# Expert stages that start with their first block, a different split of the routing, and linear attention in column halves

## The reference

```python
x = x + tanh(g_xattn[0]) * L0_xattn(layernorm(x), ctx)   # softmax attention
x = x + tanh(g_ffn[0])   * L0_ffn(layernorm(x))          # 8 experts, 2 of them per token, hidden 128
x = x + tanh(g_xattn[1]) * L1_xattn(layernorm(x), ctx)   # linear attention, 16 heads of 16, 64 features each
x = x + tanh(g_ffn[1])   * L1_ffn(layernorm(x))          # causal attention, then 16 experts, 4 per token, hidden 256

def L0_ffn(x):
    w, idx = top_k(softmax(x @ router_w), 2); w = w / sum(w)
    return sum over the chosen e of w_e * (silu(x @ gate_e) * (x @ up_e)) @ down_e

def L1_xattn(query, key, value):            # per head, per sequence of 64 tokens
    q, k = relu(q @ Wqf.T), relu(k @ Wkf.T) * mask
    kv, k_sum = k.T @ v, sum(k)             # 64 x 16 and 64
    out = (q @ kv) / (q @ k_sum + 1e-8)
```

## Time and profile before

| | us |
|---|---|
| median of three runs | 2975.49 (2974.87 to 2975.98) |
| profiled execution, its own time | 2981.3 |
| its span | 2979.5 |
| softmax attention | 0 to 742.97 |
| experts of layer 0 | 742.97 to 1030.87 |
| linear attention | 1030.87 to about 1412 |
| causal attention | about 1412 to 2360.64 |
| experts of layer 1 | 2360.64 to 2979.5 |

### The profile page before, as it was taken

How to read it: one execution, slowest core, us unless ns; L and a number is a source line. 1 busy time by engine, 2 the same in 40 slices (tenths; PEclk the granted TensorE clock), 3 DMA queues, 4 the chain that set the end, 5 groups by cost and what they waited for, 6 DMA issues and landing times. The chain is left out here.

```text
span 2979.5 us, 57684 instructions
## 1 busy us (share of the span) xinstructions
PE 2334.0 (78%) x19856; PEld 1786.5 (60%) x19856; DVE 1904.6 (64%) x3843; ACT 1108.2 (37%) x2183; POOL 1109.1 (37%) x1111
## 2 busy tenths in 40 slices
PE   4999889973496179999389999989978429999990
PEld 2555555541475168888267777777766418888770
DVE  4788778760465267776487788788777344445753
ACT  1555555542242032332244444444333233333330
POOL 2344544446305300000155444444377551002616
PEclk7777777775599589999599999999989759999995
DMA  5455555422447511111333223322233363334744
GB/s 106 111 118 100 116 114 118 96 56 75 130 153 216 164 38 38 52 39 33 114 78 83 68 68 76 82 64 69 71 87 109 114 203 120 100 98 149 234 144 138
DMA packets 249894, 308.60 MB, mean 104 GB/s; under 512 B 46104, under 2 KB 203288, under 8 KB 249496
## 3 DMA queue, kind: packets, MB, share of 16 engines
q1 hardware_dynamic: 189016, 215.29, 27.5%
q0 software_dynamic: 26624, 58.79, 7.4%
q10 hardware_dynamic: 33984, 30.95, 3.1%
HBM read 122.00 MB, written 98.43 MB: 74 GB/s over the span
## 5 line engine op out<-in xcount | busy, mean ns | idle before, releaser
L645 DVE TENSOR_REDUCE soft_top<-soft_pa 128x4 fp32r<-128x1024 f32 x256 | 312.3, 1220 | 148.8 <-PE soft_pa L728 147.4
L1834 POOL TENSOR_TENSOR ca_qk<-ca_qk,ca_q_swap 128x512 f32<-128x512 f32 x160 | 250.7, 1567 | 397.4 <-DVE ca_q_swap L2001 396.9
L1038 POOL DMA_INDIRECT moe_yg<-moe_ys_rows,moe_slot_id x192 | 194.4, 1013 | 504.4 <-DMA moe_ys_rows<-moe_ys 399.4
L555 ACT ACTIVATE soft_prob<-soft_pb 128x1024 f32<-128x1024 f32 x256 | 262.3, 1024 | 275.0 <-PE soft_pb L712 274.8
L1213 PE MATMUL moe_pgu<-moe_w_hi,moe_xt_hi 128*128 x472 | 193.2, 409 | 42.1 <-DVE moe_xt_lo L1164 39.7
L1229 PE MATMUL moe_py<-moe_w_d,moe_at 128*128 x788 | 211.4, 383 | 0.0
L728 PE MATMUL soft_pa<-soft_rep 24*128 24x256 f32 x1024 | 164.1, 407 | 46.2 <-DVE soft_top L645 36.8
L1169 DVE TENSOR_TENSOR moe_act_f<-moe_silu,moe_pgu 128x256 f32<-128x256 f32 (+1 forms) x236 | 88.7, 376 | 170.5 <-ACT moe_silu L1089 170.3
L742 PE MATMUL soft_po<-soft_prob,soft_vaug 128*32 128x256 f32 x2048 | 190.5, 506 | 0.0
L712 PEld LDWEIGHTS soft_pb<-soft_rep 25*128 25x128 f32 x1024 | 98.8, 238 | 150.2 <-ACT soft_prob L555 79.3
L712 PE MATMUL soft_pb<-soft_rep 25*128 25x256 f32 x1024 | 161.7, 402 | 34.6 <-ACT soft_prob L555 17.0
(11 more groups left out here) (363 smaller groups left out, 6472.4 us busy)
## 6 DMA issues: line engine op xcount, KB each, us to landing
ca_q_swap<-ca_q_f SPq DMA_DIRECT2D x640, 64.0 KB
moe_xs<-moe_rows SPq DMA_DIRECT2D x236, 128.0 KB, 2.1
moe_ys_rows<-moe_ys ACTq DMA_DIRECT2D x236, 128.0 KB, 2.2
soft_rep<-soft_parts SPq DMA_DIRECT2D x384, 64.0 KB
moe_rows<-soft_blank SPq DMA_DIRECT2D x27, 768.0 KB, 3.4
moe_xd<-scratch SPq DMA_DIRECT2D x64, 128.0 KB, 2.9
ca_vs<-ca_v SPq DMA_DIRECT2D x32, 256.0 KB
moe_raw<-in_L_ffn_w SPq DMA_DIRECT2D x32, 256.0 KB, 4.2
```

The lines of the kernel that those rows point to most:

```text
L555: act.activation(prob[:, k % 4, :, :], p_b[:].rearrange("p (h s) -> p h s", h=2), ACT.Exp).then_inc(prob_ready, 1)
L645: dve.tensor_reduce(heads[:, j:j + 2, :, g], p_a[:].rearrange("p (h c s) -> p h c s", h=2, c=HALF), AX, ALU.max).then_inc(a_done, 1)
L1038: pool.indirect_dma_start(out=yg[:, t % 2, k, :], out_offset=None, in_=ys_rows[h], in_offset=bass.IndirectOffsetOnAxis(ap=slot_id[:, t, k: ...
L1834: pool.tensor_tensor(qk[:, u % 2, m, :], qk[:, u % 2, m, :], q_swap[:, p % 2, :], ALU.add).then_inc(qk_ready, 1)
```

## The change

- **Split.** MOE_TILES becomes (16, 16) for moe0 and stays (20, 12) for moe1. moe0's blocks become 39 + 39. The softmax stage routes 16 tiles instead of 20, ranks them at step 22 instead of 26, and sends 32 times instead of 40: four sends in each of the steps 24 to 31 instead of six in each of steps 28 to 33 and four at the end. There and in moe0, the scaling of a tile's rows moves from DVE to ACT, with a small new DVE instruction (`centre`). Five more transfers of 768 KB clear the tensor `moe_ys`, which both expert stages now use for part two's results.
- **No prologue.** The block loop starts at once. Expert b's weights are loaded, split and waited for around block b; the constants and tables come through ACT's queue. For this, every expert gets at least one block (the threshold table's first entry becomes -1). The second part's rows are loaded once all weights are split, and its routing is spread over blocks E-1 to E+18 (moe0, E=8) or E+15 (moe1, E=16), with PSUM banks shared with `moe_py`.
- **Last gathers.** The gather ring grows from 2 to 16 tiles (moe0) and 3 (moe1). For the first 16 or 3 tiles of part two, the gathers of choice k wait only until the blocks that this choice can point to are done, with the count read from a register.
- **Linear attention.** The loop is written out. Each 128 x 128 x 68 product becomes two with 64 weight columns and 34 moving columns, on the left and on the right half of the array's columns (tile_position (0, 0) and (0, 64)); `la_den` and `la_on` become one instruction instead of two.

```diff
-MOE_TILES = (20, 12)
+MOE_TILES = {"moe0": (16, 16), "moe1": (20, 12)}
@@ softmax attention
-    ROUTED, STRETCH, SENDS = MOE_TILES[0], 4, 6
+    ROUTED, STRETCH, SENDS = MOE_TILES["moe0"][0], 4, 4
-                    if i > RANK + 1:
+                    if RANK + 1 < i < TILES:
                         if i == RANK + 2:
                             pool.wait_ge(cleared[0], 16 * CLEARS[0])
                         route.send(pool, SENDS * (i - RANK - 2), SENDS * (i - RANK - 1))
@@ expert stages
-    RAWS = 2 if MC == 1 else 4
+    RAWS = 8 // MC
+    HELD = 16 // MC ** 2 - (1 if MC == 2 else 0)
+        MEASURE, SCALE, TURN, GRADE, CHOOSE = (EXPERTS - 1 + i for i in (0, 1, 2, 4, 5))
+        RANK = CHOOSE + 3 * GROUPS
+        PLACE, MAP, WEIGH = RANK + 1, RANK + 3, RANK + 5
@@ SP
-                for b in range(3):
-                    load_rows(b)
-                for b in range(ALL):
+                for b in range(-3, ALL):
+                    if b + 3 < EXPERTS:
+                        load_w(b + 3)
                     if b + 3 < ALL:
                         load_rows(b + 3)
+                    if b + 3 < EXPERTS:
+                        load_down(b + 3)
+                    if b + 3 == EXPERTS:
+                        sp.wait_ge(wlo_ready, EXPERTS)
+                        for g in range(GROUPS):
+                            at_ = FIRST[1] + GRP * g
+                            sp.dma_start(x_new[:, GRP * g:GRP * (g + 1), :], x_in[at_:at_ + GRP].rearrange("t p d -> p t d")
+                                         ).then_inc(x_in_s[g], 16)
@@ POOL
-                fetch(0)
-                fetch(1)
+                for s in range(3):
+                    pool.wait_ge(ys_out[s], 16 * ((START[1] - s + 2) // 3))
+                for t in tiles_of(0):
+                    for k in range(TOP):
+                        gather(t, k)
+                pool.wait_ge(until_ready, 1)
+                early = list(tiles_of(1))[:HELD]
+                for k in reversed(range(TOP)):
+                    stored_to = pool.value_load(until[0:1, TOP - 1 - k:TOP - k], min_val=START[1] + 4, max_val=ALL + 3)
+                    pool.wait_ge(y_ready, stored_to)
+                    pool.tensor_tensor(spare[0:1, 0:1], route.half_neg[0:1, 0:1], route.half_neg[0:1, 0:1], ALU.add).then_inc(reached, 1)
+                    pool.wait_ge(reached, TOP - k)
+                    for t in early:
+                        gather(t, k)
+                for t in list(tiles_of(1))[HELD:]:
+                    for k in range(TOP):
+                        gather(t, k)
@@ PE
                 def up(b, e):
                     pe.wait_ge(xlo_ready, b + 1)
+                    if b < EXPERTS:
+                        pe.wait_ge(wlo_ready, b + 1)
                 def down(b, e):
+                    if b < EXPERTS:
+                        pe.wait_ge(down_in[b], 16)
                     pe.wait_ge(at_ready, b + 1)
+                    routed(b)
                     past(pe, y_ready, b - 1)
@@ linear attention, PE
-                                    mm = pe.matmul(p_kv[:, a * 4 * E:(a + 1) * 4 * E],
-                                                   kf[:, r1.slot, pair * PART:(pair + 1) * PART],
-                                                   vb[:, r1.slot, pair, :, :, :].rearrange("p b h e -> p (b h e)"),
-                                                   start=True, stop=True)
+                                    for h in range(2):
+                                        at = pair * PART + F * h
+                                        mm = pe.matmul(p_kv[F * h:F * (h + 1), a * 2 * E:(a + 1) * 2 * E], kf[:, r1.slot, at:at + F],
+                                                       vb[:, r1.slot, pair, h, :, :].rearrange("p b e -> p (b e)"),
+                                                       start=True, stop=True, tile_position=(0, F * h))
```

299 lines of the change are left out of this document (167 added, 132 removed).

## The result

| | before | changed |
|---|---|---|
| median, us | 2975.18 (four runs, 2964.9 to 2975.98) | 2860.2 (four runs, 2850.75 to 2871.58) |
| profiled execution, its own time | 2981.3 | 2850.75 |
| its span | 2979.5 | 2849.0 |

The ratio is 0.9614, with a 95% interval of 0.9584 to 0.9645: 115 us faster by the medians, 130.5 by the two profiled executions. The changed kernel's profiled execution was its fastest, so its rows flatter it; how far is taken up with the experiments.

What follows compares the result with a forecast made beforehand. No single bound: mostly the PE within stages, waits at their borders. Softmax attention -23, layer 0 -15, linear attention -30, layer 1 -68, clock +6 make -130; 2975.5 - 130 = 2845.5 us, range 2795 to 2893.

Steps and rivals of the forecast that it cites:

- the wait of 21 us at block 39: Layer 0: the PE would wait 15 to 30 us for block 39's rows, behind POOL's sends.
- In the body four tiles fewer are routed, ... -4: Softmax attention's body: fewer routed tiles and scaling moved off DVE save 4 us, between -8 and +8.
- The second part's 2.1 MB of rows: +2.5: Layer 0, blocks before block 39: loading the second part's rows adds 2.5 us.
- 16 x 2.7 + 23 x 1.75 = 83: Layer 0, part two: 16 blocks at 2.7 us, DMA-limited, and 23 at 1.75 take 83 us.
- Tail ... 45.5: Layer 0, last moe_ys to next stage: 32 gathers without waits, 41 us, begun 5 early, plus 9, make 45.5.
- 16 x 0.027 + 0.2 = 0.63: Linear attention: a group's 16 overlapping half-width passes plus shape changes take 0.63 us against 0.81, so -22 us.
- halves in turn: Linear attention: column halves don't overlap, 0.81 + 0.25 us per group, stage +22 instead of -30, total 2897; chance 0.12.
- a full drain: Linear attention: each of 256 shape changes drains the PE, 2.0 us per group, stage +144, total 3019; chance 0.02.
- 16 x 0.5 = 8, with latencies +11: Layer 1's first 16 blocks: loading and storing weights takes 3.2 us against 2.68 each, +11 us with latencies.
- Clock, +6 said: Expert stages: the granted clock was 0.87 with holes between blocks; blocks with routing or weights lose 6 us.
- weights and routing cost twice: Expert stages: slower weight transfers and routing half as dear again add 52 us, total 2897; chance 0.12.
- the routing hides: Expert stages: routing fits in DVE and ACT slack and layer 0's stall shrinks, -45 us, total 2800; chance 0.16.

Runs made afterwards that it cites:

- six_sends: Changed kernel with softmax attention sending six rows per step instead of four until the 32 are out; median 2862.7 us, ratio 0.9628 to the kernel before.
- tail_and_x_new: Changed kernel with second-part x rows loaded one group every third block and layer 0's tail loads of running sums issued two stores later; 2843.81 us, ratio 0.9562.
- la_full_width: Changed kernel with linear attention's products 128 columns wide again, with their tiles and DVE work, loop still written out; 3000.5 us, ratio 0.991 to the kernel before.
- la_in_turn: Changed kernel with all left column halves of a linear attention group first, then all right ones; 3007.56 us, ratio 0.9924 to the kernel before.

## Why the prediction was right, and where not

The forecast of 2845.5 was 14.7 us under the median and held in its range. Its sign and its main mechanisms stand; two of its terms were wrong by about 20 and by 26 us, in opposite directions, and that they cancelled is luck. Of the signs that it named, two failed: layer 0 starts at 695.2 and not at 719 to 728, and the first 16 blocks of layer 1 run at 2.7 us and not at 3.0 to 3.5. The others came: the first up products at +9.8 and +13.1, the wait of 21 us at block 39, la_pkv at 0.59, 36 gathers behind the last block.

**Softmax attention, -23 said, about -42 found.** The step that failed is "In the body four tiles fewer are routed, ... -4". I moved 706.45 by 2.6 us for two sends fewer and by these 4; in fact it moved by 28. Behind it I was near: 19.5 us forecast to the stage's end, 16.9 measured. The two runs with the old split give back 31 and 11 us of the 42, and six_sends shows that the pace of the sends isn't the cause. So the split makes much of it, and which part of the split, and what makes the rest, stays open.

**Layer 0, -15 said, +11 found.** The front came as worked out: the first up product at +9.8 (9), first send at +98.6 (98), block 39 at +143.1 (144) with a wait of 21 (23). That includes a miss of "The second part's 2.1 MB of rows: +2.5": the wait was 7.2 us. Two steps failed behind it. "16 x 2.7 + 23 x 1.75 = 83" measured 98.9. I had the DMA set the pace of the sixteen blocks with a combine; they took 46.8 us and not 43, with the DMA share at 0.78 to 0.81, held up by gathers that begin late (5.3 us of waits) and by rows that stand in SP's queue behind loads of sums that wait for a store. The five blocks behind them have the same queue ahead of their rows and took 14.3 us and not 8.8. Filling and emptying the row of blocks took some 4, which I hadn't counted, and the other blocks 2 more than 1.75 each. And "Tail ... 45.5" measured 57.1: I counted POOL's 41 us of gathers and missed the queue of sums, 2.4 us each, that holds the combines from the ninth tile on. Of the 11.6 us between, 7.3 go with SP's order (tail_and_x_new); and the gathers began 2.1 us before the last moe_ys, not 5.

**Linear attention, -30 said, -25.5 found.** The mechanism is shown twice (la_full_width, la_in_turn). The term off was "16 x 0.027 + 0.2 = 0.63", by little: a pass takes 0.029 and the two changes of shape 0.21 together, so 0.68. Part of this lies ahead of the group's first pass and behind its last, so that the 0.59 don't show it: from the last la_pk to the second la_pv it is 1.12 us against 1.25, 0.13 per group instead of 0.17, so 17 instead of 22. The rivals with halves in turn and with a full drain are out.

**Layer 1, -68 said, -68.2 found.** Front -85.8 (-88), routing with ranking 23 us (23.6), tail -14.3 (-15). Two errors cancel: "16 x 0.5 = 8, with latencies +11" is not there, the blocks with weights run at 2.7 us; I put it down to SP loading three blocks ahead, which no run tests. And the two blocks behind the last weights take 14.0 us instead of 5.4, which I had not counted; 4.6 of these 8.6 went when the x rows were spread (tail_and_x_new).

**Clock, +6 said.** Not to be told apart from the wander of softmax attention.

Of the rivals, "weights and routing cost twice" and "the routing hides" are both out: routing took about what was forecast in both stages.

## What to carry to other kernels

When work ahead of a stage is moved into it, look not only at what it adds to the blocks (here 44 us) but at which queue it puts in front of the next hand-over: 32 sends gated block 39, block 39 the first gather, and a load of a sum the next block's rows. Together this took back all 55 us of the prologue. In a tail, count the slowest ring and not the longest queue: a load that waits for a buffer's store, issued too early on the same queue, set a pace of 2.4 us where the gathers needed 1.3 each. And of a stage whose length wanders between executions by 10 us, take several profiles before a term is believed.
